# A graph attention layer on one core: each step normalises and stores the nodes that it passes, in place of an epilogue over all nodes

## The reference

```
h   = relu(layernorm(x)) @ W_node.T        # 12500 x (4 heads x 32)
e   = edge_attr @ W_edge.T
att = sum(concat(h[src], h[dst], e) * a)   # per edge and head, then leaky relu with 0.2
m   = max(segment_max(att, dst), 0)
ex  = exp(att - m[dst])
denom = segment_sum(ex, dst) + (n_edges - deg) * exp(-m)
out = x + segment_sum(ex / denom[dst] * h[src], dst)
```

## Time and profile before

| | |
|---|---|
| median of 3 runs | 2283.05 us (2278.56 to 2283.34) |
| the profiled execution's own time | 2278.08 us |
| its span, from the first to the last instruction | 2275.9 us |
| busy: PE, DVE, ACT, POOL | 61%, 62%, 40%, 70% |
| mean DMA rate | 88 GB/s |
| 1664 gathers on POOL (line 431) | 1574.4 us busy, 594.8 us idle before them |
| mean granted TensorE clock | 0.67 of full speed |

### The profile page before, as it was taken

The page is one execution under the profiler, slowest core; times in us unless marked ns, Lnnn a source line. Parts: engine busy times, 40 slices in busy tenths (PEclk is TensorE's granted clock), DMA queues, the critical chain, the costliest instruction groups (busy, mean ns, idle before and its releaser), DMA issues.

```text
span 2275.9 us, 42635 instructions
## 1 busy us (share of the span) xinstructions
PE 1384.8 (61%) x11231; PEld 1257.8 (55%) x11232; DVE 1405.3 (62%) x3802; ACT 900.0 (40%) x2278; POOL 1602.3 (70%) x1688
## 2 busy tenths in 40 slices
PE   4646566666656666666566666656665666666651
PEld 3536555565555655566555555555555555555551
DVE  5755666566666666666566566656656565665667
ACT  5523434434344343434434343443434334343440
POOL 0377777777777777777777777777777777777714
PEclk8756666656766576666666666766667666676665
DMA  7432323232232323223232332323223232322235
GB/s 207 128 92 76 93 74 94 73 94 74 75 92 75 93 75 86 82 75 93 75 93 75 76 92 74 94 74 94 73 76 92 75 94 74 94 74 75 74 86 153
DMA packets 124333, 201.16 MB, mean 88 GB/s; under 512 B 38415, under 2 KB 88799, under 8 KB 117551
## 3 DMA queue, kind: packets, MB, share of 16 engines
q0 software_dynamic: 53536, 114.27, 20.7%
q1 hardware_dynamic: 69607, 86.31, 11.9%
q10 hardware_dynamic: 1168, 0.35, 0.1%
HBM read 186.95 MB, written 13.85 MB: 88 GB/s over the span
## 4 chain that ended last, share of the span: by engine, by line
POOL 69%; issue 24%; DVE 3%; ACT 1%; PE 1%; DMA 1%; POOLq 1%; SPq 0%; DVEq 0%; ACTq 0%
POOL gath L431 69%; DVE acc L294 1%; ACT vals L872 1%; DVE gath L302 1%; SPq L316 0%; DMA gath<-in_x 0%; DVE onehot_b L660 0%; POOLq L279 0%; ACTq L872 0%; PE bank_p L1041 0%; POOLq L283 0%; DMA gath<-h_table,idx 0%; PE bank_rn L1041 0%; DVE gath L457 0%; PE bank_w L1125 0%
## 5 line engine op out<-in xcount | busy, mean ns | idle before, releaser
L431 POOL DMA_INDIRECT gath<-h_table,idx x1664 | 1574.4, 946 | 594.8 <-issue 594.8
L1090 PE MATMUL bank_t<-ident_b,onehot_b 128*128 128x128 bf16 x1688 | 186.1, 277 | 404.7 <-DVE onehot_b L660 404.3
L1125 PE MATMUL bank_p<-vals,onehot 128*128 128x137 f32 x1680 | 410.7, 437 | 0.0
L1090 PEld LDWEIGHTS bank_t<-ident_b,onehot_b 128*128 128x128 bf16 x1688 | 138.8, 126 | 445.6 <-DVE onehot_b L660 445.5
L1125 PEld LDWEIGHTS bank_p<-vals,onehot 128*128 128x128 f32 x1680 | 383.7, 329 | 0.0
L970 ACT COPY onehot_t<-bank_t 128x1024 bf16<-128x1024 bf16 x211 | 213.5, 1012 | 231.9 <-PE bank_t L1090 228.4
L1125 PE MATMUL bank_w<-vals,onehot 128*128 128x137 f32 x1680 | 304.0, 352 | 0.0
L660 DVE SCALAR_TENSOR_TENSOR onehot_b<-bank_w,base,zz 128x1024 bf16 (+1 forms) x211 | 270.9, 1284 | 41.1 <-issue 37.6
L1125 PEld LDWEIGHTS bank_w<-vals,onehot 128*128 128x128 f32 x1680 | 291.7, 257 | 3.9
L1101 PE MATMUL bank_s<-s_live,onehot_t 128*128 128x12 bf16 x3376 | 117.9, 170 | 251.8 <-ACT onehot_t L970 250.6
L1101 PEld LDWEIGHTS bank_s<-s_live,onehot_t 128*128 128x128 bf16 x3376 | 104.4, 100 | 293.7 <-issue 293.7
(11 more groups left out here) (154 smaller groups left out, 1764.6 us busy)
## 6 DMA issues: line engine op xcount, KB each, us to landing
ef<-in_edges SPq DMA_DIRECT2D x52, 1024.0 KB
gath<-h_table,idx POOLq DMA_INDIRECT x1664
gath<-in_x SPq DMA_DIRECT2D x26, 448.0 KB, 7.8
h_table<-acc SPq DMA_DIRECT2D x13, 462.0 KB
out_x<-gath SPq DMA_DIRECT2D x13, 448.0 KB
first_rows<-resets SPq DMA_DIRECT2D x208, 8.0 KB
last_rows<-resets SPq DMA_DIRECT2D x208, 8.0 KB
dst_f<-in_dst POOLq DMA_DIRECT2D x1, 832.0 KB, 8.3
```

The costliest lines, as they stand in the source:

```text
L431: e.indirect_dma_start(gath[:, q * GPS + g, t * ROW:(t + 1) * ROW], None, table, bass.IndirectOffsetOnAxis(idx[:, q, g * TILES + t:g * TIL ...
L1090: ins = e.transpose(bank_t[:, :].bitcast(BF16)[:, t * P:(t + 1) * P], onehot_b[buf][:, t, :], ident_b[:, :])
L1125: ins = e.matmul(half_p[q], onehot[q][:, t, :], vals[q][:, t, :], start=(t == 0), stop=(t == TILES - 1))
```

## The change

- Each step normalises. ScalarE takes `unseen` = exp(-m) and `others` = n_edges - degree of the `live` nodes (`den_parts`, ahead of the exponentials of `dd`). VectorE makes `den`, its reciprocal and `normed` of 128 columns (`normalise`, between the one-hot and `vals`). ScalarE splits `normed` into `flush` and `held` (`split`), then computes `ab` (`factors`), and only then widens the next one-hot. `past_window` comes after `ab_log` now; it adds `flush` to the held part of the window and adds x to two windows of 128 columns (`out_buf`). ScalarE stores these 128 KB to the output (`store`), once the store before has landed.
- x has memory of its own, `x_all`, and is not loaded again. `acc`, its clearing and the whole epilogue are gone. The node rows lie in `gath` at first, so GpSimd also waits until `s2_keep` is copied.
- SP stores all of x to the output first (`d_fill`, 14 stores of 448 KB), after the first edges; ScalarE waits for them before its first `z_places`.
- The record of VectorE has eight numbers instead of six; `d_row` says where the held part of a window is found.
- The last two steps, which have no edges, are done by `drain`, with normalisation, merge and store alone.
- In the last group only 5 of 8 tiles are gathered (1661 gathers).

The new parts of the step, as they stand in the diff (cut):

```diff
@@ gpsimd @@
             e.wait_ge(d_store, 16 * (CHUNKS + 1))
+            wait(e, n_s2, 1)
...
-                        for t in range(TILES):
+                        last = last_turn and q == RING - 1 and g == GPS - 1
+                        for t in range(LAST_TILES if last else TILES):
@@ sync @@
             load_edges(0)
+            for c in range(CHUNKS):
+                e.dma_start(x_rows(c * CHUNK, CHUNK)(out), x_all[:, c * CHUNK:(c + 1) * CHUNK, :]
+                            ).then_inc(d_fill, 16)
@@ vector: the count of steps, and the steps @@
-            chain(e.tensor_scalar(bounds[:, SUPERS:SUPERS + 1], bounds[:, SUPERS:SUPERS + 1], 3.0,
+            chain(e.tensor_scalar(bounds[:, SUPERS:SUPERS + 1], bounds[:, SUPERS:SUPERS + 1], 1.0,
...
+                    normalise(s, s_1)
                     wait(e, s_ex, s_1)
                     vh = vals[q][:, :, 0:DEG].rearrange("p t (h c) -> p t h c", c=HV)
...
+                    merge(q, s, s_1)
+                    past_window(q, (d_past0, d_past1)[q], (w_past0, w_past1)[q], s, s_1)
+
+                    rescale(q, s, s_1)
...
+            def normalise(s, s_1):
+
+                wait(e, s_ac, s_1)
+                wait(e, s_un, s_1)
+                wait(e, s_nd, s_1)
+                wait(e, s_rc, s)
+                wait(e, s_no, s)
+                e.scalar_tensor_tensor(out=den[:, :], in0=unseen[:, :], scalar=others[:, 0:1],
+                                       in1=live[:, HD:DEG:HV], op0=ALU.mult, op1=ALU.add
+                                       ).then_inc(s_dn, 1)
+                wait(e, s_dn, s_1)
+                e.reciprocal(den[:, :], den[:, :]).then_inc(s_rc, 1)
+                wait(e, s_rc, s_1)
+                wait(e, s_fn, s)
+                wait(e, s_fl, s)
+                e.tensor_tensor(
+                    normed[:, :].rearrange("p (h c) -> p h c", c=HD), per_head(live)[:, :, 0:HD],
+                    den[:, :].rearrange("p (h o) -> p h o", o=1).to_broadcast([P, HEADS, HD]),
+                    ALU.mult).then_inc(s_no, 1)
+
+            def past_window(q, d, w, s, s_1):
 
                 wait(e, s_fn, s_1)
                 wait(e, s_fl, s_1)
...
+                e.scalar_tensor_tensor(
+                    out=held[:, q, 0, :],
+                    in0=held[:, 1 - q, bass.ds(d, 1), :].rearrange("p a c -> p (a c)"),
+                    scalar=in_next[:, bass.ds(s, 1)], in1=flush[:, :], op0=ALU.mult,
+                    op1=ALU.add).then_inc(s_pt, 1)
+                wait(e, s_pt, s_1)
+                e.wait_ge(d_out, e.snap(s * 16 + 16, min_val=16, max_val=32 * PAIRS + 16))
+                e.tensor_tensor(out_buf[:, q, :, :], held[:, q, 0:2, :],
+                                x_all[:, bass.ds(w, 2), :], ALU.add).then_inc(s_ou, 1)
+
@@ scalar @@
+                    den_parts(s)
                     wait(e, s_dd, s_1)
                     e.activation(ex_p[q], dd[:, :], ACT.Exp, scale=-1.0).then_inc(s_ex, 1)
...
                     live_s2((w_b, w_c)[q], s + 3)
                     transposed(s_2)
+                    split(q, s, s_1)
+                    factors(s, s_1)
                     widened(1 - q, s, s_2)
...
+                    store(q, (w_past0, w_past1)[q], s, s_1)
...
+            def store(q, w, s, s_1):
+
+                wait(e, s_ou, s_1)
+                e.wait_ge(d_out, e.snap(s * 16 + 32, min_val=32, max_val=32 * PAIRS + 32))
+                settle(e)
+                e.dma_start(out.rearrange("(w p) d -> p w d", p=P)[:, bass.ds(w, 2), :],
+                            out_buf[:, q, :, :]).then_inc(d_out, 16)
...
-            wait(e, n_s2, 1)
-            e.wait_ge(d_store, 16 * (CHUNKS + 1))
-            e.copy(acc[:, :, :].rearrange("p w c -> p (w c)"), zero[:, :].to_broadcast(
-                [P, (WINDOWS + 2) * VALS])).then_inc(z_clear, 1)
             wait(e, n_const, N_CONST + 1)
-            wait(e, z_clear, 1)
+            e.wait_ge(d_fill, 16 * CHUNKS)
             z_places(0, 0)
```

More of the change, by code:

```diff
@@ L63 @@
 CHUNKS = WINDOWS // CHUNK
[L64 to L65 removed]
+LAST_TILES = -(-(N_EDGES - (GROUPS - 1) * GROUP) // P)
+LAST_LANDED = (GPS - 1) * TILES + LAST_TILES
 PARTS = (0, 2, 7, 10, CHUNKS)
@@ L169, in build @@
         scaled = sb("scaled", [P, DEG])
-        flush = sb("flush", [P, VALS])
+        normed = sb("normed", [P, DIM])
+        flush = sb("flush", [P, DIM])
+        held = sb("held", [P, 2, 3, DIM])
+        out_buf = sb("out_buf", [P, 2, 2, DIM])
+        unseen = sb("unseen", [P, HEADS])
+        others = sb("others", [P, 1])
+        den = sb("den", [P, HEADS])
         w_cat = sb("w_cat", [P, DIM + 2 * HEADS])
@@ L435, in _ @@
                             ).then_inc(d_gath[q], 16)
-            wait(e, f_den, 1)
-            finish(e, POOL_CHUNKS, f_pool)
+            with e.Fori(0, SUPERS // RING - 1) as i:
+                gathers(i, False)
+            gathers(SUPERS // RING - 1, True)
         @block.vector
@@ L959, in pair, with den_parts, split @@
                         beside[q][1]()
+            def den_parts(s):
+                wait(e, s_mm, s)
+                wait(e, s_dg, s)
+                wait(e, s_dn, s)
+                e.activation(unseen[:, :], live[:, MX:VALS], ACT.Exp, scale=-1.0).then_inc(s_un, 1)
+                e.activation(others[:, :], live[:, DEG:MX], ACT.Copy, bias=float(N_EDGES),
+                             scale=-1.0).then_inc(s_nd, 1)
+            def split(q, s, s_1):
+                wait(e, s_no, s_1)
+                wait(e, s_pt, s)
+                wait(e, s_ou, s)
+                settle(e)
+                e.activation(flush[:, :], normed[:, :], ACT.Copy,
+                             scale=in_this[:, bass.ds(s, 1)]).then_inc(s_fn, 1)
+                e.activation(held[:, q, 1, :], normed[:, :], ACT.Copy,
+                             scale=in_next[:, bass.ds(s, 1)]).then_inc(s_fl, 1)
@@ L1004, in _ @@
                  beside(SUPERS - 1, (SUPERS - 1) % RING * GPS))
-            s_end = walk(nc, e, bounds, SUPERS - 1, pair)
-            wait(e, s_fm, s_end)
-            wait(e, s_fl, s_end)
-            wait(e, s_b, s_end)
-            e.activation(empty, acc[:, 0:WINDOWS, MX:VALS], ACT.Exp, scale=-1.0).then_inc(f_exp, 1)
+            drain(walk(nc, e, bounds, SUPERS - 1, pair))
         @block.tensor
```

282 lines of the change are left out of this document (133 added, 149 removed).

## The result

The changed kernel takes 2246.06 us (2244.97 to 2246.99), the kernel before 2283.2 us (2278.56 to 2283.53) beside it. The ratio is 0.9842, with a 95% interval of 0.9825 to 0.9859: 1.6% faster, where 2.2% was forecast. The profiled execution of after has a span of 2244.6 us against the 2275.9 of before, 31.3 us less.

The account below looks back on a forecast made before the run. GpSimd's gathers were taken as the bound: 2275.9 - 3.75 (gathers) + 1.1 (turn) + 1.9 (four steps) + (10.0 - 62.0) (end) = 2223.2, with contention 3.5 and fill 1 2227.7 span; run time forecast 2232 us, range 2222 to 2260.

Parts of the forecast that it names:

- five signs: Profile after: gathers 0.94 to 0.96 us, `z_cols` wait 1.5 to 3.5, rescaling after 2.4, last gather 2168 to 2173, end under 58.
- Gathers set the time, steps stay hidden: Main loop: steps add 1.6 us per super (1.0 to 2.4) against 4.18 of slack, so gathers stay the bound.
- Contention on the gathers, +3.5 us (0 to 12): Gathers beside VectorE's added two-input work: the few lengthened gathers grow by about as much again, +3.5 us (0 to 12).
- My ceiling from that rule, 87 us: Skill's rule taken fully: a gather overlap with each step's 0.42 us add of x costs up to 87 us.
- The fill, 1 us (up to 12): Start: SP's fourteen stores of x, 6.4 MB, slow the first gathers by 1 us in all, bound 12.
- The step's cycle, +0.33 us: Each step: normalisation lies in VectorE's 1.37 us of idle, so the cycle grows by about 0.33 us, not 1.27.
- The record's load, +0.3 us a pair: VectorE's record load, once a pair: eight numbers instead of six add 0.3 us (0 to 0.6).
- The store: ScalarE's 128 KB result store: issue 0.38 us plus 0.1 for registers, covered by its wait; landing alone about 2.5 us.
- the slower rival: ScalarE's chain of stores sets the step from a landing of 9.5 us; 2500 us at 10.8; chance 0.04.
- The end, 54.9 us from the last gather: After the gathers: 39.3 us of old closing work gone, since normalising fits in the steps' slack; under 58 us remain.
- the turn: Last super, from `z_cols` to the first step: 9.08 us grows by 1.1; other supers' turns cost nothing.
- the contention rival: Each add of x holds a gather for 0.15 us, 208 times, +31 us, giving 2263 us; chance 0.07.

Follow-up runs that it names:

- e12: Kernel after plus three VectorE adds of 256 columns per step, one input in PSUM, behind the rescaling: 3405.21 us beside 3376.32 of before, ratio 1.0071, with pauses.
- e5: Kernel after, but ScalarE copies x's two windows into PSUM and VectorE adds them from there after the rescaling: 2233.63 us, ratio 0.9802 to before.
- e10: Kernel after without the 128 KB stores of results, a count in their place: 2236.46 us, ratio 0.9809 to before.
- e7: Kernel before plus one VectorE add of 256 columns per step, both inputs in SBUF: 3239.34 us beside 3236.62 of before, ratio 1.0006, with pauses.
- e11: Kernel before plus one 256-column VectorE add per step, both inputs in SBUF, behind the new degree: 3371.89 us beside 3385.12, ratio 0.998, with pauses.
- e2: Kernel after without the 128 KB stores of results, a count in their place: 3284.74 us beside 3247.26 of before, no interval, with pauses.
- e6: Kernel after without the 128 KB stores of results, a count in their place: 3271.18 us beside 3236.62 of before, ratio 1.0106, with pauses.
- e9: Kernel after plus three VectorE adds of 256 columns per step, one input in PSUM: 3368.04 us beside 3236.62 of before, ratio 1.0399, with pauses.

## Why the prediction was right, and where it was off

The time came out in the stated range and the path was the forecast one. Of the five signs that the prediction named, three held (the gathers' price, the wait before `z_cols`, the end) and two failed: the last gather came at 2189.3 and not by 2173, and the rescaling starts 2.78 us after ScalarE's copy and not 2.4.

- **Gathers set the time, steps stay hidden.** Right: GpSimd has no gap for a step's sake, `z_cols` still waits for SP. The idle time per super fell by 0.74 us while the super became 32 x 0.0124 = 0.40 longer, so the steps grew by 1.14 where 1.6 was forecast.
- **Contention on the gathers, +3.5 us (0 to 12).** This is the term that was mis-sized. The held-up gathers went from 2.2 us to 19.5, that is +17.3, outside my bound. I read the average (at most 10 us over 1664 gathers) as a rate per microsecond of VectorE's two-input work. Only 2.2 of these 10 us lay under such operations; the rest is 4 ns that any gather has over 0.940, and the gathers of the first 150 us. And the cost of one overlap isn't an average: it is the operation's end less 0.12 us, up to 0.26. The few two-input operations of before happened to lie where gathers rarely start. The row of 1.04 us already had this form, and laying the new operations over the gather starts of the timeline would have given the size. The Trainium skill (SBUF — State Buffer, "Who interferes with whom") states that a VectorE instruction with two SBUF inputs contends with GpSimd's reads and that whoever issues first blocks the other fully. The rows agree that the second of the two waits (1.19 us at 518.11), but not for the whole of a gather: 63 adds of x that begin 0.1 to 0.9 us behind a gather's start last 0.424 to 0.428 us, as long as with none beside them. Only the start of a gather is in conflict. My ceiling from that rule, 87 us, left out that most of the adds meet no gather's start in that way (77 do) and that only the rest of an add counts.
- **A shift of all gathers.** The forecast had no such term. A gather that nothing holds up takes some 2 ns more in after than in before (5.7 for 3.7 over 0.940; the most frequent length is 947 ns for 944), 2.4 us in all, while the gaps stayed. It appears in e12 too, and not in e5 or e10. e7 and e11 are one kernel, and the most frequent length is 947 in e7 and 944 in e11, so an edit alone doesn't decide it; but e2, e6 and e10, also one kernel, all have 944, and e9 and e12 both 947. Its cause wasn't tested. With 17.3 for the held-up gathers and 0.8 for those of the first 150 us it makes up the 20.6.
- **The fill, 1 us (up to 12).** Right. The start of the stores, a window of after (busy us and count of PE, PEld, DVE, ACT, POOL, then clock, DMA share, GB/s) and ScalarE's wait:

```profile
99.94 3.99 SPq L340 DMA_DIRECT2D out_x<-x_all  x3
...
110.00:120.00 10.00, 1.23 (x11) 1.13 (x11) 9.16 (x24) 0.00 (x0) 7.56 (x9) 0.56 1.11 334
...
128.56 0.22 ACT L925 CAST zz<-is_last 128x32 f32<-128x32 uint8 x1 [44.14 <-DMA out_x<-x_all]
```

  Its 6.4 MB were issued from 99.94 on and had landed by 128.6, some 224 GB/s, close to the 228 taken from rows 11 and a little earlier than forecast. The 334 GB/s of the window are all DMA of the core, gathers included. The first 45 gathers have 0.8 us more over 0.940 than in before (3.05 for 2.25). ScalarE's 44 us of waiting were absorbed by GpSimd's lead.
- **The step's cycle, +0.33 us.** Too small: from ScalarE's copy of the one-hot to the rescaling are now 2.78 us, 0.69 more than before. (The forecast's own terms give 2.39 - 2.09 = 0.30; the 0.33 is a slip.) The piece missed is in this timeline of after:

```profile
1121.02 1.01 ACT L1035 COPY onehot_t<-bank_t 128x1024 bf16<-128x1024 bf16 x1 [1.17 <-PE bank_t L1147]
...
1122.86 0.35 DVE L815 SCALAR_TENSOR_TENSOR held<-held,in_next,flush 128x128 f32<-128x128 f32 x1 [0.58 <-ACT flush L987]
1123.46 0.43 DVE L822 TENSOR_TENSOR out_buf<-held,x_all 128x256 f32<-128x256 f32 x1 [0.25 <-DVE held L815]
1123.80 0.35 DVE L685 SCALAR_TENSOR_TENSOR live<-live,keep,ab 128x132 f32<-128x132 f32 x1
...
1124.20 0.39 ACTq L1005 DMA_DIRECT2D out_x<-out_buf  x1
```

  `held` begins 1.84 us after the copy does, where 1.66 was forecast: 0.24 us pass between the end of ScalarE's split (1122.62) and VectorE's start, not 0.05. The add of x needs `held` and stands 0.25 us behind its end, where 0.04 was taken for dependent neighbours. The two lines in detail say what fills this time (ns min/median/max):

```profile
L821 DVEq FUSED_REGOPS  x210: 46/53/53, 154.7 to 2241.5; - x105
...
L822 DVEq FUSED_REGOPS  x210: 57/57/71, 154.8 to 2241.6; - x105
```

  Behind `held`, VectorE's queue first works out in registers the count of landed stores that it has to wait for (line 821) and then the place of the windows of x (line 822). In the step shown these begin at 1123.25 and 1123.36, and only then the add does. The forecast allowed for such register work in ScalarE's store and not here. That lay in the slack and cost nothing but in the last super. The sizes of `den`, the reciprocal, `normed` and the add (0.22, 0.18, 0.29, 0.43) were right within 0.01 us.
- **The record's load, +0.3 us a pair.** Wrong in sign: line 79 in after against rows 8.

```profile
L79 DVEq TENSOR_LOAD <-dve_rec x105: 343/635/885, 146.1 to 2233.3; - x105
```

  The median fell from 853 to 635 ns for eight numbers instead of six. So the loads gave time back, where the forecast had them take 0.6 us per super.
- **The store.** Right: 0.38 to 0.40 us to issue, 1.9 us to land, far from the 9.5 from which the slower rival decides.

```profile
out_x<-out_buf ACTq DMA_DIRECT2D x210, 128.0 KB, 1.9
```

- **The end, 54.9 us from the last gather.** 55.3 measured, but its parts cancelled: `z_cols` came 1.0 sooner than taken, the turn grew by 1.6 instead of 1.1, the four steps took 29.2 instead of 29.9, and the two shortened steps with the last store 11.6 instead of 10.0. What failed in the last is the cover of the store: without edges to work on, ScalarE stands 2.13 us until the store before has landed (the row at 2234.48) and only then makes `unseen`, and 2.01 us once more in the second of the two steps. In a full step the same landing is hidden.

In sum: 2227.7 was forecast for the span and 2244.6 measured, 16.9 more, of which the gathers have 16.1 and the first gather, later by 0.35, and the end the rest. The forecast's own range (2222 to 2245) was just missed, the whole range (2222 to 2260) held. That it was wide enough is owed to the contention rival, which had the right mechanism at nearly twice its size: it took 0.15 us for each of 208 adds, and the rows have 0.17 us for 77 of them. That the end came out within 0.4 us is luck.

## What to carry to other kernels

Where GpSimd sets the time, judge each VectorE operation added beside it by where its inputs lie, not by its length or by VectorE's slack. A second input in SBUF costs the overlapped gather the rest of that operation, so copy it to PSUM by an idle engine or place the operation so that it lies between two starts of gathers. And price such a loss by laying the operation over the starts in the timeline, not from an average.

## What the runs showed of the hardware that was not expected

The hold-up goes both ways, by which comes first. Where the add of x is recorded as beginning less than 0.05 us ahead of the gather, the add is the longer one and the gather keeps its 0.94 or 0.95:

```profile
356.76 0.49 DVE L822 TENSOR_TENSOR out_buf<-held,x_all 128x256 f32<-128x256 f32 x1 [0.25 <-DVE held L815]
356.80 0.95 POOL L398 DMA_INDIRECT gath<-h_table,idx  x1 [0.30 <-issue]
```

36 operations in after waited like this, some 1.7 us in all on VectorE, which has slack, and those gathers took no longer than the ones that nothing held up. So an add that starts 0.05 us earlier costs the bound 0.25 us, and one that starts a touch later costs it nothing. The load of eight numbers being faster than that of six, the shift of 2 ns and the pauses were not expected either, and none of them is explained.
